# Decoder layer with state-space mixer: layer norm sums as by-products of additions, squares on ScalarE

## Chip, cores and metric

One Trainium2 chip, one core. The time is device microseconds of one execution of the whole program, the median over several. The kernel before was timed three times: 5533.24, 5537.23 and 5540.6 us, median 5537.23 us. All data are fp32 except the two bfloat16 constants of the attention mask.

## What is computed

The input x has 64 sequences of 128 tokens and 512 channels. Three blocks follow each other, each fed by a layer norm without weights:

```python
def _layernorm(x, axis=-1, eps=1e-05):
    m = jnp.mean(x, axis=axis, keepdims=True)
    v = jnp.var(x, axis=axis, keepdims=True)
    return (x - m) / jnp.sqrt(v + eps)
...
x = x + _L0_attn_ref(_layernorm(x, axis=-1), ...)
x = x + _L0_xattn_ref(_layernorm(x, axis=-1), ctx_2048, ...)
x = x + _L0_ffn_ref(_layernorm(x, axis=-1), ...)
```

The first block is a state-space mixer: a projection to 1024 channels and a gate, a causal convolution over four tokens, a silu, projections to a step size and to the rows B and C, the recurrence h[t] = exp(dt*A)*h[t-1] + dt*u*B over the tokens for 1024 channels times 16 states, the sum of h*C over the states, the gate and an output projection. The second is a banded self-attention over the 512 channels as positions (8 heads of 16), with relu, a product with the context ctx and a channel projection. The third is a mixture of 8 small experts of which the router picks 2.

## The kernel before

**Stages.** Two sequences (GB = 2) form a group g; there are 32 groups (NG), and 256 tokens (NT) lie beside each other. Each engine runs a function `iteration(g, cur, nxt, p1, p2)` whose order is written out by hand, step by step. In iteration g the recurrence of group g runs (`cur`), the projections, convolution and step sizes of group g+1 are prepared (`nxt`, j = g+1), the output projection and attention of group g-1 run (`p1`), and the experts of group g-2 (`p2`). Iterations 2 to 29 are a hardware loop over two at a time.

**The recurrence.** A group has 64 steps s, each one instruction 128x512 wide per engine: `decays` (ScalarE, two Exp into one of two PSUM slots, line 462; it waits until scan s-2 is done), `times_b` (GpSimd, line 300, into a ring of 8 slots; it waits until TensorE has used the slot's last content), `scan` (VectorE, line 1454), `times_c` (24 of the 64 on VectorE, line 1439, 40 on GpSimd, line 309) and `y_sum` (TensorE, line 1066, always for two steps; it frees the ring slots). `times_b` of every sixteenth step also waits for `du`, made on VectorE by `soft_step(4, ...)` (line 1434), the last of four steps of the softplus; its other parts are `soft_exp`, `soft_one` and `soft_ln` on ScalarE. An instruction of ScalarE whose function isn't in the loaded table is preceded by an ACT_TABLE_LOAD: Exp, Ln and Silu alternate.

**The layer norms.** There are three uses, "a" (x_new, mixer of the next group), "t" (x_res, attention) and "e" (x_att, experts), each for two sequences b. `norm_stats` (VectorE, lines 1401 to 1408) takes bn_stats of the 128x512 row block, bn_aggr into `ln_mv` (mean and variance), and adds EPS into `ln_rs`. Between dependent small instructions stands `hold()`, a 128x1 copy (line 1399). `x_stats` calls it for "a"; `mixer_stats` and `experts_stats` put one more hold in front. GpSimd's `rstd` (line 288) raises to the power -0.5, VectorE's `shift` (line 1413) makes -mean*rstd, and ScalarE's `normalise` (line 469) applies both; its callers are `x_norm`, `attention_x` and `experts_norm`. The additions that make the normed tensors are `mixer_add` (line 1469, a tensor_tensor from PSUM and SBUF) and step "x2" of `attention` (line 1513, a scalar_tensor_tensor); x_new comes by DMA.

**Queues.** SyncE issues all DMAs in order. `context` (line 218) loads the tile `enc` when its last reader, step "enc" of `attention` on VectorE, is done; behind the second `context` of an iteration stand `piece(1, 6)` and `piece(0, 7)`, the weights of `gate_in(j, 2)` and `gate_in(j, 3)` on TensorE, and the write and spread of the B and C rows. x_new and x_res are loaded at the turn of two iterations, x_res when both "x2" are done. PSUM bank PS_B serves the projections of the next group, banks PS_ATT to PS_ATT+3 the attention, the output projection (`out_proj`, line 1096) and the experts. TensorE's first `attention` step "proj" (line 957) waits until `mixer_add` has read both banks of the output projection.

## Time and profile before

| | |
|---|---|
| median of three runs | 5537.23 us |
| profiled execution | 5533.42 us |
| its span, first to last instruction | 5531.6 us |
| VectorE busy | 4955.4 us (90%), 7075 instructions |
| TensorE matmul busy | 4796.2 us (87%), 51012 instructions |
| GpSimd busy | 4541.5 us (82%), 3464 instructions |
| ScalarE busy | 4058.8 us (73%), 7812 instructions |
| mean granted TensorE clock | 0.964 of full speed |
| HBM traffic | 341 MB, 62 GB/s over the span |

Busy time leaves out waits and the issue of DMAs. `copy ts` (line 561) runs once per iteration, first at 81.9 us and last at 5180.2 us, so an iteration lasts (5180.2 - 81.9) / 31 = 164.46 us. The rest, 433 us, is the first fill, one iteration and the drain of the last groups. In the rows, PE is TensorE (PEld its weight loads), DVE VectorE, ACT ScalarE, POOL GpSimd and SPq SyncE's queue; L1454 is line 1454 of the kernel.

### The profile page before, as it was taken

What the parts mean: (1) busy time and instruction counts of PE and PEld (TensorE: products, weight loads), DVE (VectorE), ACT (ScalarE), POOL (GpSimd) and SP (SyncE); (2) the same over time, 40 slices, a digit from 0 to 9 for tenths busy, and PEclk for the clock granted to TensorE, in tenths of its full rate; (3) what the DMA queues carried; (4) which work ended last, traced back from release to release, by engine and by line L of the source; (5) the groups of instructions that cost most, each with busy time, mean ns of one, the idle gap of its engine ahead of it and who ended that gap; (6) DMA issues with size and microseconds to landing.
All of it is one profiled execution on the core that took longest, in us unless ns stands there. A gap on an engine that the chain in (4) does not pass through costs nothing.

```text
span 5531.6 us, 139169 instructions
## 1 busy us (share of the span) xinstructions
PE 4796.2 (87%) x51012; PEld 3435.7 (62%) x51012; DVE 4955.4 (90%) x7075; ACT 4058.8 (73%) x7812; POOL 4541.5 (82%) x3464
## 2 busy tenths in 40 slices
PE   5788888988888988888989888989888988898876
PEld 3566666666666666666666666666666666666653
DVE  3999999999999999999999999999999999999972
ACT  3677777877777777777877777777777777777752
POOL 2988888888888888888888888888888888888870
PEclk8899999999999999999999999999999999999986
DMA  3211222221212221212221222221212221221100
GB/s 112 71 63 42 70 68 74 70 66 42 74 64 74 70 67 41 74 64 74 71 67 40 74 64 74 74 70 34 77 64 70 74 74 38 70 69 66 62 9 11
DMA packets 114693, 350.19 MB, mean 63 GB/s; under 512 B 13057, under 2 KB 14849, under 8 KB 113921
## 3 DMA queue, kind: packets, MB, share of 16 engines
q1 hardware_dynamic: 114048, 341.51, 19.0%
q8 instruction: 416, 6.82, 0.5%
q14 instruction: 229, 1.87, 0.1%
HBM read 323.64 MB, written 17.83 MB: 62 GB/s over the span
## 4 chain that ended last, share of the span: by engine, by line
PE 46%; DVE 18%; issue 15%; POOL 11%; ACT 7%; DVEq 1%; POOLq 0%; ACTq 0%
POOL ring L300 7%; PE ps L1066 7%; PE ps L1114 6%; DVE ring L1454 5%; PE ps L1096 5%; PE ps L982 4%; PE ps L957 4%; POOL ring L309 4%; PE ps L1134 3%; PE ps L1010 3%; DVE nmax L1489 3%; ACT ps L462 3%; DVE ring L1439 2%; DVE tmp L1423 2%; PE ps L1021 1%
## 5 line engine op out<-in xcount | busy, mean ns | idle before, releaser
L300 POOL TENSOR_TENSOR ring<-du,bc 128x512 f32<-128x512 f32 x2048 | 2741.9, 1356 | 577.7 <-PE ps L1066 352.3
L1454 DVE TENSOR_TENSOR_SCAN ring<-ps,ring 128x512 f32<-128x512 f32 x2048 | 2456.7, 1211 | 201.2 <-POOL ring L300 103.1
L462 ACT ACTIVATE ps<-delta,a_neg 128x254 f32<-128x254 f32 x4096 | 1761.5, 468 | 326.9 <-DVE ring L1454 320.9
L309 POOL TENSOR_TENSOR ring<-ring,bc 128x512 f32<-128x512 f32 x1280 | 1776.5, 1394 | 232.5 <-DVE ring L1454 230.6
L1066 PE MATMUL ps<-ident,ring 128*128 128x128 f32 x8192 | 1103.7, 282 | 73.7 <-DVE ring L1439 43.1
L1066 PEld LDWEIGHTS ps<-ident,ring 128*128 128x128 f32 x8192 | 962.9, 145 | 193.5 <-issue 119.1
L1439 DVE TENSOR_TENSOR ring<-ring,bc 128x512 f32<-128x512 f32 x768 | 755.4, 987 | 3.4
L592 ACT ACTIVATE probs_mem<-ps 128x768 f32<-128x768 f32 (+1 forms) x512 | 455.9, 911 | 176.0 <-PE ps L1010 174.4
L1134 PE MATMUL ps<-w_in,xt_a 128*128 128x256 f32 x2048 | 488.8, 394 | 12.8 <-DVE hc L1582 8.1
L1114 PE MATMUL ps<-xt_a,w_in 128*128 128x256 f32 x2048 | 476.6, 386 | 7.1 <-DVE hc L1582 4.1
L1096 PE MATMUL ps<-w_outp,yz 128*128 128x512 f32 x1024 | 462.5, 599 | 18.7 <-ACT yz L526 18.7
L1489 DVE TENSOR_REDUCE nmax<-ps 128x8 f32<-128x1280 f32 x256 | 380.7, 1487 | 78.4 <-PE ps L982 73.8
L1134 PEld LDWEIGHTS ps<-w_in,xt_a 128*128 128x128 f32 x2048 | 398.1, 200 | 68.4 <-DVE hc L1582 8.9
L1114 PEld LDWEIGHTS ps<-xt_a,w_in 128*128 128x128 f32 x2048 | 381.6, 191 | 76.7 <-issue 17.7
L1582 DVE SCALAR_TENSOR_TENSOR hc<-ps,conv_w,hc 128x254 f32<-128x254 f32 (+2 forms) x768 | 363.1, 473 | 62.2 <-ACT hc L537 42.7
L1096 PEld LDWEIGHTS ps<-w_outp,yz 128*128 128x128 f32 x1024 | 190.1, 191 | 227.9 <-issue 199.8
L982 PE MATMUL ps<-qk 32*32 32x160 f32 (+2 forms) x16384 | 296.2, 297 | 0.0
L1010 PE MATMUL ps<-qk 32*128 32x192 f32 (+1 forms) x4096 | 286.8, 397 | 0.0
L1021 PE MATMUL ps<-probs_mem,v_aug 128*32 128x192 f32 (+1 forms) x4096 | 229.8, 367 | 44.0 <-ACT probs_mem L592 43.9
L579 ACT ACTIVATE qk<-ps,b_qk 128x512 f32<-128x512 f32 x256 | 170.6, 678 | 125.6 <-PE ps L957 125.6
L957 PE MATMUL ps<-xb,w_qk 128*128 128x512 f32 x512 | 241.1, 593 | 2.8 <-ACT qk L579 1.3
L1010 PEld LDWEIGHTS ps<-qk 32*128 32x128 f32 x4096 | 186.3, 197 | 68.4 <-issue 63.1
(136 smaller groups left out, 6362.2 us busy)
## 6 DMA issues: line engine op xcount, KB each, us to landing
w_in<-in_w_in SPq DMA_DIRECT2D x256, 512.0 KB, 3.7
bc<-bc_rows SPq DMA_DIRECT2D x256, 512.0 KB, 4.1
x_new<-in_x SPq DMA_DIRECT2D x32, 512.0 KB, 6.2
x_res<-in_x SPq DMA_DIRECT2D x32, 512.0 KB, 5.5
enc<-in_ctx SPq DMA_DIRECT2D x64, 256.0 KB, 5.3
out<-x_att SPq DMA_DIRECT2D x32, 512.0 KB, 2.8
w_outp<-in_w_outp SPq DMA_DIRECT2D x1, 2048.0 KB, 8.0
bc_rows<-bc_sb SPq DMA_DIRECT2D x32, 32.0 KB, 1.5
```

The costliest lines, as they stand in the source:

```text
L300: nc.gpsimd.tensor_tensor(ring[:, s % RING, :].rearrange("p (n t) -> p n t", n=2), du[:, q % 2, (ic % 2) * NT:(ic % 2 + 1) * NT].rearrange ...
L309: nc.gpsimd.tensor_tensor(ring[:, s % RING, :], ring[:, s % RING, :], bc[:, s % RS, 2:4, :].rearrange("p a t -> p (a t)"), ALU.mult).then_ ...
L462: nc.scalar.activation(ps[:, s % DAR, (n % 2) * NT:(n % 2 + 1) * NT].rearrange("p (b t) -> p b t", b=GB)[:, :, 1:T], delta[:, ic, :].rearr ...
L982: last = nc.tensor.matmul(ps[32 * a:32 * a + 32, PS_ATT + hp, j * NEAR + lo:j * NEAR + hi], qk[r:r + 32, j, n * P + 32 * a:n * P + 32 * a ...
L1010: last = nc.tensor.matmul(ps[:, PS_ATT + hp, a * WIN + lo:a * WIN + hi], qk[r:r + 32, 2 + j, blk * P:(blk + 1) * P], qk[r:r + 32, j, at:at ...
L1066: last = nc.tensor.matmul(ps[:, PS_Y, b * T:(b + 1) * T], ring[:, t % RING, n * NT + b * T:n * NT + (b + 1) * T], ident[:], start=False, s ...
L1096: last = nc.tensor.matmul(ps[:, PS_ATT + b, :], yz[:, ic, b * T:(b + 1) * T], w_outp[:, ic, :], start=(ic == 0), stop=(ic == NI - 1))
L1114: last = nc.tensor.matmul(ps[:, PS_B, a * NT:(a + 1) * NT], w_in[:, slot, k, a * P:(a + 1) * P], xt_a[:, k, :], start=(k == 0), stop=(k == ...
L1134: last = nc.tensor.matmul(ps[:, PS_B, b * NT:(b + 1) * NT], xt_a[:, k, b * T:(b + 1) * T], w_in[:, slot, k, :], start=(k == 0), stop=(k == ...
L1439: nc.vector.tensor_tensor(ring[:, s % RING, :], ring[:, s % RING, :], bc[:, s % RS, 2:4, :].rearrange("p a t -> p (a t)"), ALU.mult).then_ ...
L1454: nc.vector.tensor_tensor_scan(ring[:, s % RING, :], ps[:, s % DAR, :], ring[:, s % RING, :], 0.0, ALU.mult, ALU.add).then_inc(h_done, 1)
L1489: nc.vector.tensor_reduce(nmax[:, n].rearrange("p j (a r) -> p a j r", r=32)[:, :, :, DH], ps[:, PS_ATT:PS_ATT + 4, 0:NJ * NEAR].rearrange ...
```

## The change

VectorE's statistics go: `norm_stats`, `x_stats`, `mixer_stats` and `experts_stats`, with their holds. The sum over the 512 channels comes from an accumulator output: of `mixer_add`, which becomes a scalar_tensor_tensor, for "t"; of step "x2" for "e"; and of a new ScalarE pass `total`, which copies x_new onto itself, for "a". A new ScalarE pass `squares` computes (sum - 512*x)^2 with an accumulator output. Its elementwise result is thrown away, into PSUM bank PS_B for "a", into the bank of the output projection for "t", into `enc` for "e". `variance` on ScalarE scales the accumulated value by 1/512^3 and adds EPS. `shift` reads the sum in place of the mean. Three waits move from VectorE's to ScalarE's progress: `context` waits for `squares` of use "e", TensorE's first "proj" for both `squares` of use "t", and `squares` of use "a" waits for the last users of PS_B.

```diff
-        ln_st = {k: sb("ln_st_" + k, [P, GB, 6]) for k in "ate"}
-        ln_mv = {k: sb("ln_mv_" + k, [P, GB, 2]) for k in "ate"}
+        eps = sb("eps", [P, 1])
+        ln_sum = {k: sb("ln_sum_" + k, [P, GB]) for k in "ate"}
+        ln_var = {k: sb("ln_var_" + k, [P, GB]) for k in "ate"}
...
             def context(i):
-                reached(sp, enc_used, i)
+                reached(sp, ln_aggr["e"], i)
...
+            def total(j, b):
+                act.wait_ge(x_in, (j + 1) * 16)
+                nc.scalar.activation(x_new[:, b, :], x_new[:, b, :], ACT.Identity,
+                                     accum_out=ln_sum["a"][:, b:b + 1]).then_inc(ln_stat["a"], 1)
+
+            def squares(use, g, b):
+
+                i = g * GB + b
+                if use == "a":
+                    reached(act, yz_done, (g - 1) * NI)
+                    reached(act, gate_done, g * NQ)
+                    if b:
+                        act.wait_ge(ln_aggr["a"], i)
+                src = {"a": x_new, "t": x_res, "e": x_att}[use]
+                act.wait_ge({"a": ln_stat["a"], "t": x1_done, "e": x2_done}[use], i + 1)
+                nc.scalar.activation({"a": ps[:, PS_B, :], "t": ps[:, PS_ATT + b, :], "e": enc[:]}[use], src[:, b, :], ACT.Square,
+                                     scale=-float(H), bias=ln_sum[use][:, b:b + 1],
+                                     accum_out=ln_var[use][:, b:b + 1]).then_inc(ln_aggr[use], 1)
+
+            def variance(use, g, b):
+                act.wait_ge(ln_aggr[use], g * GB + b + 1)
+                nc.scalar.activation(ln_rs[use][:, b:b + 1], ln_var[use][:, b:b + 1], ACT.Identity,
+                                     scale=1.0 / H ** 3, bias=eps[:]).then_inc(ln_eps[use], 1)
...
-                        pe.wait_ge(x1_done, g * GB)
+                        pe.wait_ge(ln_aggr["t"], g * GB)
...
-                nc.vector.tensor_tensor(x_res[:, b, :], ps[:, PS_ATT + b, :], x_res[:, b, :], ALU.add).then_inc(x1_done, 1)
...
+                nc.vector.scalar_tensor_tensor(x_res[:, b, :], ps[:, PS_ATT + b, :], 1.0, x_res[:, b, :], ALU.mult, ALU.add,
+                                               accum_out=ln_sum["t"][:, b:b + 1]).then_inc(x1_done, 1)
...
-                                                   ALU.add, ALU.add).then_inc(x2_done, 1)
+                                                   ALU.add, ALU.add, accum_out=ln_sum["e"][:, b:b + 1]).then_inc(x2_done, 1)
```

Two copies in the router that wrote a tile now write a column of `held`, in equal number. The hand-written order of GpSimd, ScalarE, TensorE and VectorE is new throughout; the order of SyncE's DMAs isn't. What the text below speaks of:

- ScalarE, new order at the start of an iteration: decays 2, experts_norm, total 0, decays 3, total 1, decays 4, gate_raw, decays 5, experts_x twice, y_back, soft_one, squares a 0, skip_term, decays 6, squares t 0, decays 7, squares a 1, variance t 0, router_exp, decays 8, variance a 0, decays 9, soft_ln, variance a 1, experts_silu, attention_x 0, squares t 1, decays 10.
- ScalarE, the calls of Silu: `u_silu` 0, 1 and 2 and both `gate_silu` stand together behind decays 43; `u_silu(j, 3)` stands alone between two Exp of the attention. Before, two `u_silu` and one `gate_silu` stood together in two places, and `soft_ln(g, 3)` came directly behind the first of them.
- ScalarE, end: squares e 0 behind decays 56, variance e 0 behind decays 61, squares e 1 behind decays 62, variance e 1 last.
- VectorE: `soft_step(4, g, 1)` from behind scan 14 to behind scan 4; `soft_step(4, g, 2)` from behind scan 25 to behind scan 20; `soft_step(4, g, 3)` from behind scan 46 to ahead of scan 43; `shift("t", g - 1, 1)` from behind scan 15 to behind scan 21.
- TensorE: `gate_in(j, 2)` from behind step 59's y_sum to ahead of step 57's; the second sequence's first scores from behind gate_in(j, 0) to behind step 33's y_sum.

## Rows read from the trace of the kernel before

**Rows 1.** The page: the chain that ended last, shares by engine.

```profile
PE 46%; DVE 18%; issue 15%; POOL 11%; ACT 7%; DVEq 1%; POOLq 0%; ACTq 0%
```

**Rows 2.** Busy time by stretch: us, PE, PEld, DVE, ACT, POOL (instructions), clock, DMA share, GB/s.

```profile
81.90:5180.20 5098.30, 4502.27 (x48074) 3243.50 (x48078) 4729.76 (x6710) 3878.23 (x7484) 4367.98 (x3323) 0.98 0.20 65
2400.00:2500.00 100.00, 91.22 (x1079) 64.10 (x1077) 94.54 (x148) 71.81 (x143) 89.85 (x71) 1.00 0.19 64
```

**Rows 3.** VectorE's groups: operation, tiles, shapes, count, busy us, mean ns, idle before.

```profile
L1399 DVE COPY held<-neg_half 128x1 f32<-128x1 f32 x416 | 62.1, 149 | 10.1
...
L1403 DVE BATCH_NORM_STATS2 ln_st_t<-x_res 128x6 f32<-128x512 f32 x64 | 43.7, 683 | 0.0
...
L1406 DVE BATCH_NORM_AGGREGATE ln_mv_t<-ln_st_t 128x2 f32<-128x6 f32 x64 | 11.0, 172 | 0.0
L1408 DVE TENSOR_SCALAR ln_rs_t<-ln_mv_t 128x1 f32<-128x1 f32 x64 | 9.8, 154 | 2.2
```

**Rows 4.** VectorE's timeline over one statistic: start us, us, operation.

```profile
2542.95 0.13 DVE L1399 COPY held<-neg_half 128x1 f32<-128x1 f32 x1
...
2544.10 0.69 DVE L1439 TENSOR_TENSOR ring<-ring,bc 128x512 f32<-128x512 f32 x1
```

**Rows 5.** VectorE's groups, the two additions.

```profile
L1513 DVE SCALAR_TENSOR_TENSOR x_att<-ps,b_ct,x_res 128x512 f32<-128x512 f32 x64 | 46.9, 733 | 4.1 <-PE ps L1050 4.1
...
L1469 DVE TENSOR_TENSOR x_res<-ps,x_res 128x512 f32<-128x512 f32 x64 | 43.3, 677 | 6.8 <-PE ps L1096 6.8
```

**Rows 6.** ScalarE's groups nearest to the added work.

```profile
L579 ACT ACTIVATE qk<-ps,b_qk 128x512 f32<-128x512 f32 x256 | 170.6, 678 | 125.6 <-PE ps L957 125.6
...
L512 ACT ACT_TABLE_LOAD x128 | 164.2, 1283 | 2.2
...
L506 ACT ACTIVATE tmp<-soft 128x512 f32<-128x512 f32 x128 | 80.4, 628 | 57.1 <-DVE delta L1426 56.0
...
L469 ACT ACTIVATE x_new<-x_new,ln_nm_a,ln_rs_a 128x512 f32<-128x512 f32 x64 | 51.8, 811 | 3.8 <-DVE ln_nm_a L1413 3.8
...
L605 ACT ACTIVATE small<-small 128x16 f32<-128x16 f32 x32 | 6.9, 216 | 132.8 <-DVE small L1538 132.8
```

**Rows 7.** Who waited for whom: engine, line, releaser: us in total, times, longest.

```profile
DVE ring L1454 <- POOL ring L300: 103.1, 129, 4.8
DVE ring L1454 <- ACT ps L462: 94.2, 95, 3.0
...
PE ps L944 <- ACT probs_mem L592: 78.4, 40, 3.3
...
PE ps L1021 <- ACT probs_mem L592: 43.9, 63, 2.7
...
POOL ring L300 <- DVE du L1434: 225.4, 96, 77.1
```

**Rows 8.** TensorE's timeline around the first projection of an attention.

```profile
2417.18 7.11 PE L1096 MATMUL ps<-w_outp,yz 128*128 128x512 f32 x16
...
2426.10 1.88 PE L957 MATMUL ps<-xb,w_qk 128*128 128x512 f32 x4
```

**Rows 9.** VectorE's timeline, the addition between the two.

```profile
2424.54 0.68 DVE L1469 TENSOR_TENSOR x_res<-ps,x_res 128x512 f32<-128x512 f32 x1
```

**Rows 10.** Timeline of SyncE's queue: weights of gate_in(j, 2) and (j, 3), then x_new.

```profile
2512.43 6.14 SPq L207 DMA_DIRECT2D w_in<-in_w_in  x2
...
2563.11 0.40 SPq L226 DMA_DIRECT2D x_new<-in_x  x1
```

**Rows 11.** TensorE's timeline: gate_in(j, 2), which needs the first of the two weights.

```profile
2558.08 3.62 PE L1134 MATMUL ps<-w_in,xt_a 128*128 128x256 f32 x16
```

**Rows 12.** ScalarE's timeline: decays 56 of one iteration, decays 2 of the next.

```profile
2540.03 0.87 ACT L462 ACTIVATE ps<-delta,a_neg 128x254 f32<-128x254 f32 x2
...
2570.78 0.85 ACT L462 ACTIVATE ps<-delta,a_neg 128x254 f32<-128x254 f32 x2
```

**Rows 13.** The page's DMA issues: count, KB each, median us to landing.

```profile
x_new<-in_x SPq DMA_DIRECT2D x32, 512.0 KB, 6.2
```

More of the change, by code:

```diff
@@ L643, in iteration @@
                     decays(g, 8)
+                if nxt:
+                    variance("a", g + 1, 0)
+                if cur:
+                    decays(g, 9)
                     soft_ln(g, 2)
+                if nxt:
+                    variance("a", g + 1, 1)
                 if p2:
                     experts_silu(g - 2)
-                if cur:
-                    decays(g, 9)
                 if p1:
                     attention_x(g - 1, 0)
+                    squares("t", g - 1, 1)
                 if cur:
@@ L757, in iteration @@
                     decays(g, 36)
+                if p1:
+                    attention(g, p2, 1, "qk", 0)
+                if cur:
                     decays(g, 37)
+                if p1:
+                    attention(g, p2, 1, "qk", 1)
+                if cur:
+                    decays(g, 38)
+                if p1:
+                    attention(g, p2, 1, "qk", 2)
                 if nxt:
@@ L1218, in iteration @@
                     experts_up(g - 2)
+                if cur:
+                    y_sum(g, 7)
                 if p1:
@@ L1222, in iteration @@
                 if cur:
[L1223 removed]
+                    y_sum(g, 9)
                 if p1:
@@ L1271, in iteration @@
                     attention(g, p2, 0, "rep")
-                    attention(g, p2, 1, "proj", 0)
                 if cur:
@@ L1275, in iteration @@
                 if p1:
+                    attention(g, p2, 1, "proj", 0)
                     attention(g, p2, 0, "wo")
@@ L1278, in iteration @@
                     y_sum(g, 27)
+                    y_turn(g, 2, nxt)
+                if nxt:
+                    gate_in(j, 0, cur)
+                if cur:
+                    y_sum(g, 29)
+                if nxt:
+                    h_in(j, 2, cur)
+                if cur:
+                    y_sum(g, 31)
                 if p1:
@@ L1325, in iteration @@
                 if cur:
+                    y_sum(g, 43)
+                if p1:
+                    attention(g, p2, 1, "st", 2)
+                if cur:
                     y_turn(g, 4, nxt)
+                    y_sum(g, 45)
+                if p1:
+                    attention(g, p2, 1, "st", 3)
+                if cur:
+                    y_sum(g, 47)
                 if nxt:
@@ L1329, in iteration @@
                 if p1:
-                    attention(g, p2, 1, "st", 2)
-                if cur:
-                    y_sum(g, 47)
+                    attention(g, p2, 1, "av", 1)
                 if nxt:
@@ L1704, in iteration @@
                 if cur:
+                    scan(g, 28)
+                    times_c(g, 25)
+                    soft_step(1, g, 3)
+                    scan(g, 29)
                     y_step(g, 2)
-                    scan(g, 28)
                 if p1:
@@ L1770, in iteration @@
                 if cur:
-                    times_c(g, 44)
-                    soft_step(4, g, 3)
+                    scan(g, 47)
+                    scan(g, 48)
                 if nxt:
@@ L1804, in iteration @@
                 if cur:
-                    y_step(g, 6)
                     scan(g, 59)
+                if nxt:
+                    soft_step(2, j, 0)
+                if cur:
+                    scan(g, 60)
+                    times_c(g, 57)
                 if p1:
```

563 lines of the change are left out of this document (260 added, 303 removed).

## The prediction, made before the changed kernel ran

> **What bounds the kernel now.** I read the shares of the engines first, by stretch. In the 31 iterations between 81.9 and 5180.2 us VectorE is busy 4729.76 of 5098.30 us, 93%; TensorE 88%, GpSimd 86%, ScalarE 76% [rows 2]. Per iteration of 164.46 us that is 152.6, 145.2, 140.9 and 125.1 us. So VectorE is the fullest engine and ScalarE the emptiest, and the change moves work from the one to the other. But TensorE stands only 7 us behind VectorE, and the chain that ended last runs over TensorE for 46% and over VectorE for 18% [rows 1]. A stretch of 100 us from one iteration shows the same: TensorE is busy 91.22 us and VectorE 94.54 [rows 2]. No engine is the bound alone; whoever is late makes the others wait. VectorE idles 11.9 us of an iteration, TensorE 19.3. The reader is to see in the waits that VectorE's scan waits about as long for GpSimd's products (103.1 us in all) as for ScalarE's decays (94.2 us) [rows 7].
>
> **What the change removes.** Six statistics per iteration leave VectorE. Each has bn_stats 683 ns, bn_aggr 172, the EPS addition 154 and one or two holds of 149 [rows 3]; with their overlap, the timeline shows 2544.10 - 2542.95 = 1.15 us from the first hold to the next work [rows 4]. The ten holds that go are the larger part of 13 per iteration (416 in all over 32 [rows 3]). 6 x 1.15 = 6.9 us per iteration.
>
> **What it adds on VectorE.** `mixer_add` becomes a scalar_tensor_tensor: 733 against 677 ns, twice, 0.11 us [rows 5]. Four additions write an accumulator out, which no row shows. Below, nothing (a by-product); above, twice a small copy of 149 ns [rows 3], 0.3 us each. I take 0.1 us, nearest to the copy less its overlap with its neighbour: 0.4 us, ends 0 and 1.2 us. Here the Trainium skill (VectorE: DVE Perf Modes, section "Two Vector instructions with no wait between them") speaks for a cost: an op that also writes out its accumulator is two instructions. By it four small instructions of 149 ns come to 0.6 us in place of 0.4, some 6 us over the kernel. Net relief of VectorE: 6.9 - 0.1 - 0.4 = 6.4 us per iteration; over 32 groups 205 us.
>
> **What it adds on ScalarE.** Two `total` passes at 628 ns (an Identity 128x512 without pointers) are 1.3 us. Six `squares` lie between the one-pointer Identity from PSUM, 678 ns, and the two-pointer one, 811 ns; I take 0.72: 4.3 us. Six `variance` at 216 ns (128x16) to 0.3: 1.8 us. Eight accumulator outputs, between 0 and 0.3 us each; I take 0.2, near the 216 ns of the smallest activation: 1.6 us [rows 6]. And one table load more. Before, Ln stands in four places of an iteration and Silu in three, in five stretches of other functions than Exp: 7 loads in and 5 back to Exp, 12. In the new order `soft_ln(g, 3)` stands alone and `u_silu(j, 3)` too: six stretches, 7 loads in and 6 back, 13, at 1283 ns [rows 6]. Sum 10.3 us, ends 7 and 13: ScalarE goes from 125.1 to 135 us per iteration. That is still 10 us under VectorE's new 146.2, so it costs nothing as a total. What hides it is ScalarE's lead of two scans over VectorE in the decays; where that lead is used up, each late decay delays a scan.
>
> **What moves.** `soft_step(4, ...)` comes two to ten scans earlier. GpSimd waited 225.4 us for it, 77.1 of them once at the start [rows 7], so 4.6 us per iteration. GpSimd isn't the bound, and its products wait for ring slots as well; I count 0.4 us per iteration for it, ends 0 and 1.5. The later second attention and the earlier gate_in I count at nothing: they are the same instructions, hidden beside the recurrence; without that cover each score step of about 1.5 us would stand on TensorE's path.
>
> **The new waits.** First, TensorE's "proj" waited for the second `mixer_add`. TensorE ends its output projection at 2417.18 + 7.11 = 2424.29 us, the addition runs at 2424.54 to 2425.22, and the projection starts at 2426.10 [rows 8, 9], after two y_sum and a transpose: 0.9 us of slack. Now `squares` t 1 (0.72, and about 0.2 for its accumulator, and a semaphore hop more) stands between, behind attention_x in ScalarE's queue. Queued behind "proj" are the experts' last matmuls, the second "proj" and y_sum 7. I take 0.7 us of stall per iteration, ends 0 and 2.5. Second, `context` for the second sequence now waits for `squares` e 0, behind decays 56. Queued behind it on SyncE are piece(1, 6), which before went out at 2512.43 [rows 10], piece(0, 7) and the B and C rows. Decays 56 run at 2540.03 in this iteration [rows 12], so with `squares` and a load as long as that of x_new, 6.2 us [rows 13], the weights are there at about 2548; gate_in(j, 2) runs at 2558.08 [rows 11]. The new order asks for it ahead of two y_sum, some 4 us earlier, so a margin of 10 us shrinks to some 5, and I count nothing; if it goes, gate_in and the three y_sum behind it are late by what is missing. Third, ScalarE's `total` waits for x_new: issued at 2563.11 [rows 10], it lands at 2569.3 [rows 13], and `total` stands behind decays 2, which run at 2570.78 [rows 12]. The issue hangs on the second "x2", which in the new order has two more steps of the softplus and one more product between it and the next scan, and a statistic less, so I count nothing here too.
>
> **The sum.** Per iteration -6.4 (VectorE) -0.4 (du) +0.7 (proj). Two shares are given back. TensorE waits for ScalarE: two of the largest rows are 78.4 and 43.9 us, 122.3 together, 3.8 us per iteration [rows 7]. ScalarE's filling goes from 76% to 135/160 = 84%, so its answers come later; I take a third more, 1.3 us. And VectorE's two-source operations meet GpSimd's more often in a shorter iteration: 0.4 us. Together -4.4 us per iteration. Over 32 groups -141 us; with the few us that fill and drain save, -150 us, or 160 us per iteration. Against the profiled execution of 5533 us this gives 5383; it lies 4 us under the median of the three runs, so the median forecast is about 5385 us, 2.7% faster.
>
> **The rivals.** (1) VectorE is the bound after all and the new order gives up nothing. For it: it is the fullest engine, and every wait of another engine on it gets shorter with it. Against it: the chain's 46% on TensorE [rows 1]. Then 5537 - 205 - 0.4 x 32 = 5319 us; at the bounds of the du term 5285. (2) TensorE is the bound: in that stretch of 100 us it idles only 8.8 us [rows 2], and nothing of its own work is removed. If its idle time of 19.3 us can shrink by no more than 2 us, the kernel gains about 64 us: 5473 us. (3) ScalarE's queue turns the sign. The place is the scan's wait for its decays, 94.2 us now, 2.9 us per iteration [rows 7]. The stretch from router_exp to decays 10 holds three table loads and a normalisation, and now two `variance` and one `squares` more. If the decays come late in that stretch and at the end (squares e 1, variance, Ln), the wait grows; it decides from the point where each of the 64 scans waits 0.1 us more on average, which eats the 6.4 us. At 0.13 us it gives +2 us per iteration: 5600 us. Such a loss would be certain if Square weren't in the tables that hold Exp: some eleven table loads more, 11 x 1.283 = 14 us of ScalarE per iteration, most of them ahead of a decay, about +2.5 us after the relief, 5620 us. The Trainium skill (ScalarE: Activation LUTs, section "Table sets: the hidden batching unit") says that cheap functions such as copy, identity and abs are in every set. The trace agrees for these three (Abs, Identity and Copy run among Exp without a load); it shows no Square. (4) The change doesn't do what it says: the accumulators are no saving if their read-out costs 1.15 us an addition. The upper bound above is a quarter of that, so I give it nothing of its own.
>
> **How the numbers follow.** Forecast 0.5 (5330 to 5440), rival 1 0.24, rival 2 0.13, rival 3 0.13. A measurement of this kernel tells 0.2%, 11 us, from no change. Faster: the forecast, rival 1 and most of rival 2, 0.82; within 0.2%: the end of rival 2, 0.05; slower: rival 3, 0.13. The range takes in rival 1 to its lower values and rival 2: 5290 to 5490 us. It leaves out rival 3 and a little below.
>
> **What would show it.** Right: bn_stats and bn_aggr gone, VectorE's instructions 28 fewer per iteration (24 if each accumulator output is one), its busy time near 4750 us; ScalarE near 4390 us with 13 table loads per iteration (416 in all) and Square without a load of its own; iterations of about 160 us; TensorE above 90% in them; "proj" waiting under 1 us for `squares`. Wrong: a scan's wait for decays of over 200 us in all (rival 3), TensorE unchanged in its idle time (rival 2), loads of w_in that gate_in waits for, or table loads beyond 500.

## The result, and the profile after

The changed kernel takes 5588.29 us in the median of four runs (5574.74 to 5591.58); the kernel before, on the same chip, 5535.23 us. The ratio is 1.0091, interval 1.0071 to 1.0110: 0.9% slower, where 2.7% faster was forecast and the range ended at 5490 us. From the starts of the scans in the trace, an iteration of the full pipeline (the 4th to the 31st) lasts 166.95 us; before it lasted 165.54. (The profiled executions took 5591.58 and 5533.42 us.)

The page of the changed kernel, busy time and the chain, which answers to [rows 1]:

```profile
PE 4780.5 (86%) x51012; PEld 3417.1 (61%) x51012; DVE 4811.0 (86%) x6307; ACT 4323.4 (77%) x8548; POOL 4594.7 (82%) x3465
...
POOL 29%; PE 23%; issue 19%; DVE 12%; ACT 11%; DMA 2%; SPq 1%; POOLq 0%; DVEq 0%; ACTq 0%
```

Its groups by line, engine and form, which answer to [rows 5] and [rows 6] (count, busy us, mean ns of one, idle before):

```profile
L1511 DVE SCALAR_TENSOR_TENSOR x_res<-ps,x_res 128x512 f32<-128x512 f32 x64 | 43.9, 686 | 31.2 <-PE ps L1149 31.1
L1511 DVE DVE_READ_ACCUMULATOR x_res<-ps,x_res 128x1 f32 x64 | 5.3, 82 | 0.0
L1476 DVE TENSOR_TENSOR du<-delta,u 128x512 f32<-128x512 f32 x128 | 138.9, 1085 | 0.0
L1472 DVE TENSOR_TENSOR delta<-delta,lnv 128x512 f32<-128x512 f32 x128 | 137.1, 1071 | 0.6 <-ACT lnv L540 0.6
L485 ACT ACTIVATE enc<-x_att,ln_sum_e 128x512 f32<-128x512 f32 x64 | 45.4, 710 | 13.3 <-DVE x_att L1542 13.3
L485 ACT ACTIVATION_READ_ACCUMULATOR ps<-x_new,ln_sum_a 128x1 f32 x64 | 12.7, 198 | 0.0
L491 ACT ACTIVATE ln_rs_t<-ln_var_t,eps 128x1 f32<-128x1 f32 x64 | 18.5, 288 | 0.0
L1010 PE MATMUL ps<-xb,w_qk 128*128 128x512 f32 x512 | 257.6, 616 | 41.4 <-ACT qk L607 25.4 <-ACT ps L485 15.3
```

The parts that the change names came out near their prices. The statistics are gone and VectorE is busy 144.4 us less (4955.4 to 4811.0), where 205 was forecast. `du` and `delta` ran in 696 and 697 ns before and take 1085 and 1071 ns at their new places, 4 each in an iteration; that is 3.1 us, 98 us in all. Others got shorter at theirs: the product that makes `tmp` (1364 to 1020 ns, 44 us in all) and one product of the router (784 to 175 ns, 20 us). ScalarE is busy 8.3 us per iteration more (4058.8 to 4323.4 in all), where 10.3 were forecast. The accumulator of an addition is read out in 82 ns. Squares take 710 ns and a read-out on ScalarE 198. Square brings no table load of its own. "proj" waits 15.3 us for `squares`, 0.5 us per iteration. TensorE, whose work is the same, is 15.7 us less busy; its mean granted clock is 0.971, before 0.964. And still the kernel is slower, so the cost is in waits. Here are those of the changed kernel that grew, and last the one that fell:

```profile
POOL ring L302 <- PE ps L1119: 609.2, 335, 4.3
DVE ring L1496 <- ACT ps L465: 310.1, 293, 5.4
PE ps L981 <- DVE nmax L1518: 136.7, 151, 1.9
DVE nmax L1518 <- PE ps L1035: 133.5, 170, 4.3
PE ps L997 <- DVE qk L1525: 74.1, 64, 1.3
POOL ring L302 <- DVE du L1476: 78.8, 4, 74.5
```

The wait of the scan for its decays has more than tripled from the 94.2 us of [rows 7], beyond the 200 us that the prediction set as the mark of rival 3. The wait for `du` has fallen from 225.4 to 78.8 us, as the move of `soft_step(4, ...)` was to bring; GpSimd now waits for TensorE's y_sum instead (352.3 to 609.2 us). TensorE waits for attention's maxima (136.7 us, before 72.3) and for `qk` (74.1, before 12.7). The reader is to see one thing: most of these waits sit between steps that the change only moved.

### The profile page after: what moved, and what is told of

The parts are those of the page before. It is cut to its first block, busy times and chain, and to the rows that moved or that the text cites. A ratio compares the mean times of both kernels' runs of the same rounds, so it can differ in the third digit from the quotient of the medians.

```text
span 5589.7 us, 139231 instructions
## 1 busy us (share of the span) xinstructions
PE 4780.5 (86%) x51012; PEld 3417.1 (61%) x51012; DVE 4811.0 (86%) x6307; ACT 4323.4 (77%) x8548; POOL 4594.7 (82%) x3465
## 4 chain that ended last, share of the span: by engine, by line
POOL 29%; PE 23%; issue 19%; DVE 12%; ACT 11%; DMA 2%; SPq 1%; POOLq 0%; DVEq 0%; ACTq 0%
POOL ring L302 18%; POOL ring L311 11%; DVE ring L1496 4%; ACT ps L465 3%; PE ps L1119 3%; PE ps L1063 3%; PE ps L1167 3%; DVE nmax L1518 2%; DMA bc<-bc_rows 2%; PE ps L1196 2%; PE ps L1202 2%; PE ps L1074 2%; ACT probs_mem L620 2%; PE ps L1035 2%; PE ps L1187 2%
## 5 line engine op out<-in xcount | busy, mean ns | idle before, releaser
L302 POOL TENSOR_TENSOR ring<-du,bc 128x512 f32<-128x512 f32 x2048 | 2787.1, 1377 | 703.0 <-PE ps L1119 609.2
L1496 DVE TENSOR_TENSOR_SCAN ring<-ps,ring 128x512 f32<-128x512 f32 x2048 | 2459.0, 1211 | 322.6 <-ACT ps L465 310.1
L1119 PE MATMUL ps<-ident,ring 128*128 128x128 f32 x8192 | 1092.9, 280 | 82.0 <-DVE ring L1481 58.1
L1119 PEld LDWEIGHTS ps<-ident,ring 128*128 128x128 f32 x8192 | 951.2, 144 | 220.0 <-issue 177.6
L1518 DVE TENSOR_REDUCE nmax<-ps 128x8 f32<-128x1280 f32 x256 | 380.7, 1487 | 133.5 <-PE ps L1035 133.5
L1010 PE MATMUL ps<-xb,w_qk 128*128 128x512 f32 x512 | 257.6, 616 | 41.4 <-ACT qk L607 25.4
L997 PE MATMUL ps<-band,ident_bf 32*32 32x512 bf16 x4096 | 116.5, 399 | 187.9 <-ACT probs_mem L620 74.7
L1035 PEld LDWEIGHTS ps<-qk 32*32 32x32 f32 x16384 | 205.5, 105 | 40.3 <-issue 4.1
```

The source lines that it names most:

```text
L302: nc.gpsimd.tensor_tensor(ring[:, s % RING, :].rearrange("p (n t) -> p n t", n=2), du[:, q % 2, (ic % 2) * NT:(ic % 2 + 1) * NT].rearrange ...
L1035: last = nc.tensor.matmul(ps[32 * a:32 * a + 32, PS_ATT + hp, j * NEAR + lo:j * NEAR + hi], qk[r:r + 32, j, n * P + 32 * a:n * P + 32 * a ...
L1119: last = nc.tensor.matmul(ps[:, PS_Y, b * T:(b + 1) * T], ring[:, t % RING, n * NT + b * T:n * NT + (b + 1) * T], ident[:], start=False, s ...
L1496: nc.vector.tensor_tensor_scan(ring[:, s % RING, :], ps[:, s % DAR, :], ring[:, s % RING, :], 0.0, ALU.mult, ALU.add).then_inc(h_done, 1)
L1518: nc.vector.tensor_reduce(nmax[:, n].rearrange("p j (a r) -> p a j r", r=32)[:, :, :, DH], ps[:, PS_ATT:PS_ATT + 4, 0:NJ * NEAR].rearrange ...
```

## Experiments

The kernel before ran beside each; its medians were 5530.7, 5530.7, 5535.1, 5530.9 and 5531.9 us.

**Taking the change apart.** Two kernels cross the parts. In the first the sums come from accumulators and `squares` and `variance` stand on ScalarE, but the four orders of work are the old ones. In the second the orders are the new ones and the statistics stay on VectorE. Where the moved steps stand among the others had to be chosen in both. The router's two copies into `held` go with the statistics: the first kernel has them, the second has the old ones.

```diff
# e1_stats_old_order: new statistics, every iteration() as before, with
+                    squares("a", g + 1, 0)       # behind experts_x(g - 2, 0)
+                    squares("t", g - 1, 0)       # behind decays 6
+                    variance("t", g - 1, 0)      # ahead of router_exp
+                    squares("e", g - 1, 1)       # behind decays 63
# e2_order_old_stats: the changed kernel's iteration() on each engine, with
-                    squares("t", g - 1, 0)
+                    mixer_stats(g - 1, 0)        # VectorE, behind x_stats(j, 1)
+                    experts_stats(g - 1, 0)      # VectorE, behind scan 56
```

> The new statistics in the old order: accumulators, total, squares and variance as in the changed kernel, and every other step of all four engines where it stood before; squares of use e stand early, behind decays 37 and 63. Theory O (the new order is what costs, the statistics themselves gain or are neutral): at or below the time of before, 5450 to 5535 us. Theory S (ScalarE's ten added microseconds per iteration make the decays late, whatever the order): slower than before by 1% or more, 5590 to 5700 us, with the scan's wait for its decays far above 94 us. Theory B (VectorE was never worth relieving, both shifts nearly free): within 0.3% of before.

> The new order of the four engines with VectorE's old statistics put back at the places they had before (behind scan 3, behind the two mixer additions, behind scan 56 and in the last steps). Theory O: slower than before by as much as the changed kernel or more, 5590 to 5750 us, since VectorE's 6.9 us come on top. Theory S: near before or a little above, 5530 to 5580 us, since ScalarE has its old load. Theory B: the time is set by TensorE and GpSimd's ring: near the changed kernel, 5570 to 5600 us.

| median, us | old order | new order |
|---|---|---|
| statistics on VectorE | 5531 | 5730 |
| statistics by accumulators | 5897 | 5588 |

The ratios to the kernel before are 1.0662 (1.0644 to 1.0680) for the statistics alone and 1.0363 (1.0345 to 1.0380) for the order alone. Each half alone is a large loss; together they are 0.9%. Inside the new order the statistics are worth 5730 - 5588 = 142 us or 4.4 us per iteration. The order itself costs 199 us, 6.2 per iteration, measured with the old statistics; with the new ones it gains 309 us. So neither half has a price of its own, and the sum of the two single costs (199 + 366) says nothing about the whole. TensorE's clock is part of both losses: the mean granted clock is 0.954 in the first kernel and 0.957 in the second (0.964 before, 0.971 with both halves), and for the same 51012 matmuls TensorE is busy 4881.0 and 4844.6 us (4796.2 before). The waits of the second kernel, with VectorE's statistics in the new order:

```profile
DVE ring L1452 <- ACT ps L462: 256.4, 212, 4.7
PE ps L928 <- DVE nmax L1487: 141.2, 152, 1.9
DVE nmax L1487 <- PE ps L982: 147.6, 171, 4.3
PE ps L944 <- DVE qk L1494: 74.6, 64, 1.3
PE ps L1066 <- DVE ring L1437: 141.0, 93, 4.6
```

The first four are those of the changed kernel (310.1, 136.7, 133.5, 74.1) with no `squares` anywhere, so the order makes most of them, not ScalarE's new work. The fifth, TensorE waiting for VectorE's products, is 43.1 us before and 58.1 in the changed kernel. The first kernel has other waits:

```profile
POOL ln_rs_a L290 <- ACT ln_rs_a L491: 252.5, 32, 20.9
PE ps L971 <- DVE probs_mem L1609: 145.0, 30, 4.9
```

and, among its groups,

```profile
L1600 DVE TENSOR_TENSOR small<-iota,small 128x16 f32<-128x16 f32 x64 | 70.7, 1144 | 1.1
```

GpSimd's `rstd` of "a" stands early in the old order and there waits for ScalarE's `variance` in every iteration, once 20.9 us and otherwise 7.5 in the mean, with the products queued behind it. The wait for `probs_mem` and the group are taken up below.

**ScalarE's passes and the held queue.** In one kernel the squares for the experts write into `xb` and SyncE's `context` waits as before; in another `total` and `squares` run over one column and the variance is a constant, so the sums leave most of the row out.

```diff
# e3_context_early
-                reached(sp, ln_aggr["e"], i)
+                reached(sp, enc_used, i)
# e6_short_passes
-                nc.scalar.activation({... "e": enc[:]}[use], src[:, b, :], ACT.Square,
+                nc.scalar.activation({... "e": enc[:, 0:1]}[use], src[:, b, 0:1], ACT.Square,
```

> The changed kernel, but squares of use e write their discarded result into xb in place of enc, so the context load waits for its old reader again and SyncE's queue isn't held for decays 56. Theory Q (the held queue bunches the loads at the turn of the iteration: the spreads of B and C landed in 5.4 us in place of 4.1, x_new in 8.4 in place of 6.2, and gate_in waits for its weights): faster than the changed kernel by 20 to 60 us, 5530 to 5570 us, and those landings back at 4.1 and 6.2 us. Theories O, S and B: the same time within 10 us, 5580 to 5600 us.

> The changed kernel with total and squares on one column in place of 512 (and the variance a constant 1): the same instructions, order and waits, ScalarE 8 x about 0.43 = 3.4 us lighter per iteration, 110 us in all. If ScalarE's added load is what gives the gain back (theory S): 5480 to 5520 us, and the scan's wait for its decays well under 310 us. If the order itself holds the time (theory O) or the bound is elsewhere (theory B): 5570 to 5590 us.

They took 5584.45 us (1.0096, 1.0079 to 1.0113) and 5577.58 us (1.0088, 1.0071 to 1.0105). ScalarE is busy 4224.6 us instead of 4323.4 in the second, yet the scan still waits 299.3 us for decays. The held queue is out as a cause: without it the kernel gains 4 us. ScalarE's longer passes are worth little: 99 of its 265 us of added work gone give 11 us. The accumulator outputs, `variance` and the thirteenth table load stay in this kernel.

**Single places of the new order.** The changed kernel's trace has a visible hole: VectorE idles 3.09 us before scan 51 (2.85 in the mean of 27 full iterations), for decays that stand behind a table load, `u_silu`, another load and two exps of the attention.

```profile
2546.53 1.28 ACT L572 ACT_TABLE_LOAD   x1
2547.83 0.63 ACT L572 ACTIVATE u<-hc 128x512 f32<-128x512 f32 x1
2548.47 1.28 ACT L620 ACT_TABLE_LOAD   x1
2549.77 1.73 ACT L620 ACTIVATE probs_mem<-ps 128x1024 f32<-128x1024 f32 x2
2551.38 0.87 ACT L465 ACTIVATE ps<-delta,a_neg 128x254 f32<-128x254 f32 x2
```

One kernel puts these decays ahead of the exps; one asks for the maxima sooner on VectorE; a third is the second with three products moved from GpSimd to VectorE as well.

```diff
# e14_decays_first (ScalarE)
+                    decays(g, 51)                # ahead of exps 6 and 7
# e16_maxima_sooner (VectorE, and the same around scan 41)
                     scan(g, 15)
+                    attention(g, 0, "max", 3)
                     times_c(g, 12)
...
-                    attention(g, 0, "max", 3)    # stood behind soft_step(3, g, 2)
# e17_three_products_moved: times_c 14, 30 and 46 on VectorE
```

> The changed kernel with decays 51 moved ahead of the attention's exp 6 and 7, which in the new order stand with the lone u_silu 3 and its two table loads between decays 50 and 51; VectorE waited 3.1 us there in the iteration that was looked at. If that stall is on the path that sets the iteration: faster than the changed kernel by 1 to 1.6 us per iteration, 5535 to 5560 us. If it is made good later in the iteration by the ring: 5580 to 5590 us.

> The changed kernel with VectorE's maxima of the attention scores moved ahead: the fourth of the first sequence directly behind scan 15 (it stood behind two products, a scan and a step of the softplus), the third and fourth of the second sequence one scan earlier. If TensorE's waits for the maxima and the shifted queries are what the new order costs: 1 to 3 us per iteration faster than the changed kernel, 5490 to 5555 us. If those waits only stand in for others: 5575 to 5600 us.

> As the one before, and three of GpSimd's products with C per iteration (steps 14, 30 and 46) are done by VectorE, in all 27 on VectorE and 37 on GpSimd: about 4 us off GpSimd, 2 to 4 us onto VectorE, which the change relieved by 4.5. If GpSimd's ring is what VectorE's relief should feed: 10 to 40 us faster than the one before. If VectorE is full again at once, as added statistics showed in the old order: slower by 20 to 80 us.

5591.27 us (1.0102, 1.0085 to 1.0118); 5670.19 us (1.0250, 1.0231 to 1.0269); 5757.95 us (1.0404, 1.0387 to 1.0421). Moving the decays closes the hole only to open another: before scan 51 the idle time falls from 2.85 to 1.14 us, before scan 52 it grows from 0.27 to 1.94. Both edits to VectorE's order lose, and the mean granted clock falls with them, from 0.971 to 0.960 and 0.949. Earlier maxima didn't shorten TensorE's waits (139.9 us for `nmax` against 136.7, and 139.1 for `qk` against 74.1).

**What relief of each engine is worth in the old order.** This is the step on which the whole sum stood. Each kernel is the one before with one engine's work cut: VectorE's six bn_stats, bn_aggr and ten holds are left out (mean and variance are constants); eight of GpSimd's forty `times_c` multiply 128 columns instead of 512; Ln is replaced by Exp, so that its table loads go; then these three together.

```diff
# e5_relief_alone
-                nc.vector.bn_stats(ln_st[use][:, b, :], src[:, b, :]).then_inc(ln_stat[use], 1)
-                hold()
-                nc.vector.bn_aggr(ln_mv[use][:, b, :], ln_st[use][:, b, :]).then_inc(ln_aggr[use], 1)
# e9_gpsimd_relief
+                w = 128 if s % 8 == 3 else 2 * NT
# e10_no_ln_tables
-                nc.scalar.activation(lnv[:], soft[:], ACT.Ln, bias=1.0).then_inc(sp_ln, 1)
+                nc.scalar.activation(lnv[:], soft[:], ACT.Exp, bias=1.0).then_inc(sp_ln, 1)
# e13_three_reliefs: all three
```

> The kernel before, with bn_stats, bn_aggr and their ten holds per iteration taken out and the mean and variance of every layer norm a constant 1 (the addition of EPS, the power, the shift and the norm remain). Nothing is added on ScalarE. It prices VectorE's relief alone in the old order, about 5.9 us per iteration. The prediction's step (relief of VectorE shortens the iteration one for one): 5345 to 5370 us. If TensorE or the ring through GpSimd is as much the bound (theory B): 5480 to 5530 us.

> The kernel before with eight of GpSimd's 40 products with C (steps 3, 11, 19 and so on) on 128 columns in place of 512: about 7 us of GpSimd less per iteration, the other columns of those steps stay without C. If GpSimd is the bound: 5310 to 5400 us. Theory B1 (TensorE): within 0.5% of before. Theory B2: 5450 to 5530 us.

> The kernel before with Exp in place of the four Ln per iteration (the step size is then wrong in value): table loads fall from 12 to about 4 per iteration, some 9 us of ScalarE. ScalarE is the emptiest engine. If its occupancy doesn't matter (the prediction's view that the added load costs nothing as a total): within 0.5% of before. If the in-order queue ahead of the decays matters (theory S): 5350 to 5480 us.

> The kernel before with three reliefs at once: no statistics on VectorE (mean and variance a constant 1), Exp for Ln on ScalarE, and eight of GpSimd's products with C on 128 columns. Alone they gave nothing, nothing and 27 us. If each was hidden by the next engine (a ring of near equals without TensorE): together far more than their sum, 5300 to 5420 us. If TensorE and the waits around it set the pace (theory B1): no more than the sum, 5480 to 5510 us.

| relief | median, us | ratio and interval |
|---|---|---|
| VectorE | 5534.42 | 1.0007 (0.9997 to 1.0016) |
| GpSimd | 5503.71 | 0.9947 (0.9931 to 0.9964) |
| ScalarE, Ln | 5527.71 | 0.9991 (0.9982 to 1.0001) |
| all three | 5498.91 | 0.9937 (0.9921 to 0.9954) |

VectorE's relief alone, its busy times on the page and then its waits:

```profile
PE 4803.9 (87%) x51012; PEld 3443.7 (62%) x51012; DVE 4802.5 (87%) x6371; ACT 4064.0 (73%) x7812; POOL 4565.5 (83%) x3467
```

```profile
DVE ring L1450 <- ACT ps L464: 123.8, 154, 2.7
DVE nmax L1483 <- PE ps L984: 110.7, 101, 4.3
DVE small L1526 <- PE ps L1179: 54.5, 32, 11.2
```

VectorE is busy 153 us less and the kernel takes the same time. Time has gone into VectorE's own waits: 123.8 us for decays (94.2 before), 110.7 for attention's scores (73.8), 54.5 for the router's logits (11.3). This is the clearest result of the study: all of the relief becomes idle time.

**What more work costs.** VectorE gets each bn_stats twice; TensorE adds four of the eight channel blocks of its output projection twice, in the old order and in the new. (Only block 0 starts a sum, so the doubled blocks are counted twice in the result; the third expectation below is wrong where it calls the results the same.)

```diff
# e12_vector_more
+                nc.vector.bn_stats(dup[:, b, :], src[:, b, :])
# e11_tensor_more (before), e20_tensor_more_new_order (the changed kernel)
-                for ic in range(lo, hi):
+                for ic in [c for c in range(lo, hi) for _ in range(2 if c in (1, 2, 3, 5) else 1)]:
```

> The kernel before with each of the six bn_stats per iteration run twice (the first result is discarded): 4 us of VectorE more per iteration, where taking 4.8 us away gave nothing. If VectorE has slack to both sides (theory B1): 5530 to 5570 us. If the iteration is set by VectorE as soon as it gets heavier: 5620 to 5670 us. Half of that if it binds only in the stretch behind scan 56.

> The kernel before with 16 matmuls of 128x512 more per iteration in the output projection (four of eight channel blocks are summed twice): about 7 us of TensorE added, where leaving the same 16 out made the kernel slower by 2.8% and the granted clock fall from 0.964 to 0.934. If TensorE is the bound in that stretch (theory B1): 7 us per iteration, 5740 to 5770 us. If TensorE has slack there (theory B2): 5540 to 5620 us.

> The changed kernel with sixteen out_proj matmuls more in each iteration (7 us of TensorE; their results are the same, since they write the same sums again from the start). In the old order the same addition cost 178 us, 5.6 of 7 us in each iteration. If TensorE sets the pace in the new order too: 150 to 220 us over the changed kernel, 5740 to 5810 us. If waits between engines that TensorE takes part in only now and then (the decays, the maxima) set it, part of the 7 us hides in TensorE's idle time of 20.2 us: under 100 us over, below 5690 us.

VectorE: 5692.75 us (1.0283, 1.0266 to 1.0300), 158 us for 4 us of work per iteration, which is 4.9 per iteration. TensorE: 5712.75 us (1.0324, 1.0307 to 1.0341), 178 us or 5.6 of 7 us per iteration. TensorE in the new order: 5816.87 us, 229 us over the changed kernel, 7.1 per iteration. Work added to TensorE costs nearly in full, in the new order too. For VectorE the 158 us can't be read as a price: kernels with less TensorE work fall onto the same time, as the next part shows, and this one has their marks too.

**Less work on TensorE.** Channel blocks of the output projection are left out: one (4 of 32 matmuls per iteration, 1.8 us), two, four, and four with the three reliefs above.

```diff
-                for ic in range(lo, hi):
+                for ic in [c for c in range(lo, hi) if c != 1]:            # e18_one_block_out
# e19_two_blocks_out: without 1 and 2; e8_tensor_relief and e15_four_reliefs: without 1, 2, 3 and 5
```

> The kernel before with half of the output projection's matmuls left out (four of eight channel blocks are not summed): 16 matmuls of 128x512 fewer per iteration, about 7 us of TensorE. It prices TensorE's relief in the old order as the kernel without statistics priced VectorE's (which was nothing). If TensorE is the bound of the kernel before (theory B1): 5310 to 5400 us. If no single engine is (theory B2, a ring of waits between all of them, set by the latency of each step): 5450 to 5530 us.

> The three reliefs together (constant mean and variance without VectorE's statistics, Exp for Ln, eight products with C on 128 columns) and half of the output projection's matmuls left out. With three it was 5499 us. If TensorE's work sets the pace and only waits for the others made its own relief useless (theory B1): 5300 to 5420 us. If the gaps that open on TensorE lower its granted clock and that takes back what the work gives (theory C): 5480 to 5640 us, with a mean clock under 0.95 and dips at fixed places of each iteration.

> The kernel before without the out_proj matmuls of one channel block (4 of 32 in each iteration, some 1.8 us of TensorE each iteration, 56 us over 32). The block's contribution is left out of the sum. If TensorE's own work sets the pace and nothing else answers: 1.4 to 1.8 us less in each iteration, 5475 to 5490 us. If another engine sets it: within 10 us of the kernel before (5531). If the gap opened here is enough to bring the granted clock down at further places, as with sixteen matmuls left out (5686 us at a mean clock of 0.934): over 5545 us, with a mean clock under 0.960.

> The same with two channel blocks left out (8 of 32 matmuls, some 3.5 us in each iteration, 112 us over 32). TensorE sets the pace and nothing else answers: 5420 to 5450 us. Another engine sets it: within 10 us of 5531. The clock answers: over 5560 us, mean clock under 0.955, and the time grows from one block to two to four (5686), a cost that rises with the work left out. If one and two blocks gain and only four lose, the loss of four belongs to what it opened at its own places.

| left out | median, us | ratio and interval | mean granted clock |
|---|---|---|---|
| one block | 5524.38 | 0.9988 (0.9979 to 0.9998) | 0.964 |
| two blocks | 5689.97 | 1.0283 (1.0266 to 1.0300) | 0.952 |
| four blocks | 5686.48 | 1.0281 (1.0264 to 1.0298) | 0.934 |
| four, and three reliefs | 5672.73 | 1.0258 (1.0241 to 1.0275) | 0.943 |

One block gives 7 of 56 us. The second costs 166 us, and the third and fourth nothing more: a step, not a slope. From the starts of the scans an iteration (the 4th to the 30th) lasts 165.40 us before and 165.24 with one block out. With two blocks out it lasts 170.66 us, with four 170.67, with four and the three reliefs 170.66, and with bn_stats twice 170.66: four kernels of different work, one length. From scan 0 to scan 16 of an iteration 44.4 us pass before, 49.5 with two blocks out, 50.0 with four and 49.3 with bn_stats twice; the rest of the iteration differs from before by less than 0.5 us. What steps? One wait of TensorE, with four blocks out and then with two:

```profile
PE ps L912 <- DVE probs_mem L1572: 147.4, 32, 4.8
```

```profile
PE ps L912 <- DVE probs_mem L1572: 109.8, 31, 3.9
```

Before, and with one block out, this wait is 3.9 us in all, once. With bn_stats twice it is there too, 52.1 us in 30 times. TensorE's L912 transposes the experts' gates, the end of VectorE's `router` chain of short dependent operations. Here are the timelines (start us, us, operation), first of the kernel before, VectorE in that chain and then GpSimd; then with four blocks out, VectorE, GpSimd and TensorE:

```profile
2421.00 0.83 DVE L1547 TENSOR_TENSOR small<-small 128x16 f32<-128x16 f32 x1
2421.87 0.15 DVE L1399 COPY held<-neg_half 128x1 f32<-128x1 f32 x1
2421.94 0.23 DVE L1552 MAX8 small<-small 128x8 f32<-128x8 f32 x2
2422.08 0.16 DVE L1553 COPY small<-small 128x16 f32<-128x16 f32 x1
...
2422.63 0.15 DVE L1558 COPY small<-small 128x16 f32<-128x16 f32 x1
2422.82 0.17 DVE L1560 CAST small<-small 128x4 f32<-128x4 uint32 x1
...
2420.53 1.27 POOL L309 TENSOR_TENSOR ring<-ring,bc 128x512 f32<-128x512 f32 x1
2424.82 1.28 POOL L300 TENSOR_TENSOR ring<-du,bc 128x512 f32<-128x512 f32 x1 [3.01 <-PE ps L1066]
```

```profile
2486.15 0.97 DVE L1553 COPY small<-small 128x16 f32<-128x16 f32 x1
...
2487.50 0.83 DVE L1558 COPY small<-small 128x16 f32<-128x16 f32 x1
2488.37 1.18 DVE L1560 CAST small<-small 128x4 f32<-128x4 uint32 x1
...
2485.81 1.28 POOL L300 TENSOR_TENSOR ring<-du,bc 128x512 f32<-128x512 f32 x1
2487.03 1.27 POOL L309 TENSOR_TENSOR ring<-ring,bc 128x512 f32<-128x512 f32 x1
2488.25 1.28 POOL L300 TENSOR_TENSOR ring<-du,bc 128x512 f32<-128x512 f32 x1
...
2481.33 3.68 PE L1096 MATMUL ps<-w_outp,yz 128*128 128x512 f32 x8
2484.85 1.04 PE L1066 MATMUL ps<-ident,ring 128*128 128x128 f32 x8
2490.65 0.69 PE L912 MATMUL ps<-ident,probs_mem 128*128 128x128 f32 x2 [4.77 <-DVE probs_mem L1572]
```

Before, TensorE's output projection of 7.11 us [rows 8] holds back a y_sum, the y_sum holds back the ring slot, and GpSimd stands idle for 3.01 us. In just that gap VectorE's router runs, at 0.15 to 0.17 us a piece; only the product at its start, under GpSimd's last one, takes 0.83. With a shorter output projection the y_sum comes sooner, GpSimd goes on without a gap, and three more of the router's operations take 0.97, 0.83 and 1.18 us, each ending 0.02 to 0.03 us after GpSimd's product (2486.15 + 0.97 = 2487.12, and 2485.81 + 1.28 = 2487.09). TensorE, in order, waits 4.77 us for the end of the chain with the y_sum behind it. So the time that was taken from TensorE opened GpSimd's queue onto a chain of VectorE that TensorE waits for. Over an iteration the router's operations, with the copy that ends the chain, sum to 3.98 us before and with one block out, 6.76 with two, 6.32 with four, and 6.66 in the kernel with the new statistics in the old order, whose row is shown above (1144 ns where the same operation had 172); TensorE's wait there is 145.0 us. With bn_stats twice they sum to 5.06 us, and it is the end of the chain that is long:

```profile
L1574 DVE COPY probs_mem<-small 128x256 f32<-128x256 f32 x32 | 38.1, 1189 | 1.1
```

This copy takes 294 ns before. The link is read from the traces; no run moved the router alone.

The Trainium skill (SBUF — State Buffer, section "Who interferes with whom") states that VectorE and GpSimd share a port pair that is locked for a whole instruction, and that copies and casts can take part in this, and operations with two inputs from SBUF. The trace agrees: copies, the cast and tensor_tensor are stretched, the 128x1 hold and MAX8 beside them are not (0.15 us, and 0.23 for two).

The mean granted clock, 0.964 in the old kernel, falls with two and four blocks out to 0.952 and 0.934: more of the span has the lower level of 1.2 GHz. Part of this sits right behind the router. With four blocks out, the stretch in which TensorE waits for the chain and the one after it (us, PE, PEld, DVE, ACT, POOL, clock, DMA share, GB/s):

```profile
2486.00:2490.60 4.60, 0.00 (x0) 0.00 (x0) 4.39 (x17) 4.56 (x9) 3.53 (x3) 0.76 0.00 0
2490.60:2493.00 2.40, 2.35 (x10) 1.97 (x11) 2.40 (x5) 0.78 (x3) 0.00 (x0) 0.50 0.00 0
```

TensorE does nothing for 4.60 us, its granted clock falls to 0.50 of full speed within that time, and the first projection behind it takes 2.95 us, where it took 1.88 [rows 8]. The clock falls at this place (behind scan 8 or 9) in each of the 27 iterations with two and with four blocks out, with four blocks and three reliefs out, with bn_stats twice, and with the new statistics in the old order; in the kernel before, with one block out and with more TensorE work it never falls there. An estimate of what the clock costs: leaving out one block makes TensorE 40.4 us less busy (4796.2 to 4755.8), but leaving out the second makes it 26.4 us busier (4782.2), so some 67 us of TensorE's time went to the lower level, beside the 166 us that the second block cost. The cascade is then: the chain is late, TensorE idles, and then works at half speed. Router and clock come together in these traces, so their shares were not separated, and what holds four different kernels at 170.66 us is not shown.

## Why the prediction was wrong

**The step that failed** is the first term of the sum, "-6.4 (VectorE)", counted in full as time because VectorE was the fullest engine. In the old order a relief of 4.8 us of busy time per iteration, three quarters of the term, is worth 0 us (5534.42 against 5530.7), where the term counts 205 for the whole. The prediction itself had "No engine is the bound alone; whoever is late makes the others wait" and then priced as if one were.

**The second step that failed** is "The later second attention and the earlier gate_in I count at nothing: they are the same instructions, hidden beside the recurrence". With `du` at -0.4 and proj at +0.7 the order was priced near nothing; it measures +6.2 us per iteration with the old statistics, clock included. This is the step that turned the sign: +6.2 for the order and -4.4 for the statistics in it make the +1.8 us per iteration that was measured (58 us against the kernel before in the same runs), where -4.4 was forecast. The price that the prediction named for the case of lost cover, score steps on TensorE's path, is in the trace as the waits for `nmax` and `qk` (72.3 to 136.7 and 12.7 to 74.1 us), and the decays' wait comes with them.

**What was right.** In the new order the change of the statistics is worth 4.4 us per iteration. That this is the very figure of the sum is luck: the sum had the order in it, and no run shows why the statistics are worth that much there. VectorE's instructions are 24 fewer per iteration, ScalarE's table loads 13, Square needs none, "proj" waits 0.5 us against 0.7, the accumulators cost 0.08 us each on VectorE (0.1 taken) and 0.19 to 0.20 on ScalarE (0.2 taken). The term for VectorE meeting GpSimd, 0.4 us, had been worked out for a shorter iteration and not for moved steps: `du` and `delta` alone grew by 3.1 us, while `tmp` and the router's product fell by 2.0. SyncE's queue and `total` were rightly at nothing.

**The rivals.** Rival 1 (VectorE the bound) is refuted by the relief alone. Rival 2 (TensorE the bound) had the nearest mechanism: added TensorE work costs 5.6 to 7.1 of 7 us. It is still not the whole, since less work on TensorE gains almost nothing or loses. Rival 3 named the sign and the place, the scan's wait for decays over 200 us, but with the wrong cause: it blamed ScalarE's added work, of which 99 of 265 us taken away give 11 us, and the wait is 256.4 us without any of it. Its 13% were too few because slower cases in which the order alone loses had no share.

**What stays open.** Which of the moved steps makes the 6.2 us was not found, nor on which engine they stand: the three edits tried at single places gained nothing or lost, and no run has the new order on one engine alone. How much of any of these losses is TensorE's clock was not separated either. The new statistics in the old order lose 366 us with two large waits and the fall of the clock behind the router, not split. No version tried with the full computation beats the kernel before.

## What to carry to other kernels

In a kernel like this one, where four in-order engines all stand above 70%, price a relief at nothing until the chain shows that every engine it feeds could come sooner too; a fast test is to cut the work and look whether the time moves, before building what replaces it. Don't read a price from one such test either: here less work on TensorE and more on VectorE gave the same +2.8%. Comparing iteration length and granted clock across the tests shows whether they all fell onto the same step. Price a reordering as an edit of its own, by moving the steps with the old operations. And before an engine is made faster, look at which idle gap of GpSimd a chain of short VectorE operations lives in: the gap may be what the slow engine was giving.

## What the runs showed of the hardware

- A short VectorE operation of 0.15 to 0.17 us (copy 128x16, cast 128x4, tensor_tensor 128x16) takes 0.83 to 1.18 us when a GpSimd product of 1.27 us is under way. Holds, MAX8 and FIND_INDEX8 between them are not stretched.
- With four blocks out TensorE's idle time of 4.77 us behind the router ends with its granted clock at 0.50, the level of 1.2 GHz; four matmuls of 128x512 soon behind it take 2.95 us (granted clock 0.63 over their stretch), where they take 1.88 at full clock.
- An accumulator output of VectorE is a separate record of 82 to 83 ns. The Trainium skill (VectorE: DVE Perf Modes, section "Two Vector instructions with no wait between them") says that such an operation is two instructions, and the trace agrees. The scalar_tensor_tensor that feeds it is no slower than the tensor_tensor was (686 against 677 ns). ScalarE's takes 187 to 198 ns.
- The response is not smooth: leaving out one block (4 matmuls per iteration, 1.8 us) gives -0.1% and two blocks +2.8%, and four kernels of different work have iterations of 170.66 or 170.67 us. A sum of small terms can't see such a step.
